# Expert products of a routed SwiGLU layer with the weights as the stationary operand

## What is computed

```python
T, D, F, E, TOP_K = 2048, 256, 1024, 8, 2
probs = softmax(x @ gate_w)                       # T x E
weights, experts = top_k(probs, TOP_K); weights /= weights.sum(-1)
for i in range(E):
    wi = where(experts == i, weights, 0).sum(-1)
    h = silu(x @ w1[i]) * (x @ w3[i])             # T x F
    out += (h @ w2[i]) * wi[..., None]
```

## Time and profile before

| | |
|---|---|
| runs | 791.32, 793.56, 793.77 us; median 793.56 us |
| the profiled execution | 792.24 us, of which the span of instructions is 790.5 us |
| mean granted TensorE clock | 0.901 |
| routed tiles | from 420 us to 777 us of the span |

### The profile page before, as it was taken

How to read it: one execution, slowest core, us unless ns; L and a number is a source line. 1 busy time by engine, 2 the same in 40 slices (tenths; PEclk the granted TensorE clock), 3 DMA queues, 4 the chain that set the end, 5 groups by cost and what they waited for, 6 DMA issues and landing times.

```text
span 790.5 us, 16899 instructions
## 1 busy us (share of the span) xinstructions
PE 656.0 (83%) x4582; PEld 456.3 (58%) x4582; DVE 505.7 (64%) x1269; ACT 383.9 (49%) x894; POOL 277.6 (35%) x297
## 2 busy tenths in 40 slices
PE   3899999995765775577317999999999999999991
PEld 2788888873323335477313666666666666666661
DVE  6588999997687456688693464646464555564441
ACT  1466666655869335476224443645353545443320
POOL 3111111220354402544202363637364545563311
PEclk9899999998898997555557999999999999999997
DMA  9100000003000006111371514262434353512214
GB/s 283 37 14 13 13 14 14 7 0 106 2 0 0 1 9 230 30 34 27 127 247 29 187 28 139 77 182 47 135 81 133 83 147 81 188 28 35 35 15 119
DMA packets 45682, 58.89 MB, mean 74 GB/s; under 512 B 13296, under 2 KB 39216, under 8 KB 45328
## 3 DMA queue, kind: packets, MB, share of 16 engines
q1 hardware_dynamic: 38128, 47.79, 18.5%
q0 software_dynamic: 7488, 10.31, 7.5%
HBM read 145.90 MB, written 11.80 MB: 199 GB/s over the span
## 4 chain that ended last, share of the span: by engine, by line
PE 56%; DVE 18%; issue 10%; ACT 5%; DMA 4%; POOL 3%; DVEq 2%; ACTq 1%; SPq 0%; POOLq 0%
PE psum L1000 19%; PE psum L1022 10%; PE psum L708 4%; PE psum L1013 3%; PE psum L692 3%; PE psum L715 3%; PE psum L728 2%; ACT region L1271 2%; PE psum L697 1%; PE psum L747 1%; DMA region<-neg_max_dram 1%; PE psum L735 1%; DVE region L1893 1%; POOL region L590 1%; PE psum L891 1%
## 5 line engine op out<-in xcount | busy, mean ns | idle before, releaser
L1000 PE MATMUL psum<-region 128*128 x936 | 217.1, 382 | 1.0 <-DVE region L1889 1.0
L1000 PEld LDWEIGHTS psum<-region 128*128 128x128 bf16 x936 | 92.2, 98 | 96.5 <-issue 4.1
L1254 ACT ACTIVATE region<-psum 128x512 f32<-128x512 f32 x78 | 46.5, 596 | 182.0 <-PE psum L1000 182.0
L636 POOL DMA_INDIRECT sum_dram<-region,row_token x39 | 74.5, 1911 | 133.7 <-DVE region L1885 133.7
L1022 PE MATMUL psum<-region 128*128 x936 | 109.1, 273 | 5.6 <-DVE region L1893 5.6
L1022 PEld LDWEIGHTS psum<-region 128*128 128x128 bf16 x936 | 90.4, 98 | 18.8 <-issue 8.2
L1868 DVE TENSOR_TENSOR region<-psum,region 128x512 f32<-128x512 f32 x78 | 53.9, 691 | 69.9 <-ACT region L1254 69.8
L529 POOL TENSOR_TENSOR region<-region,pair_mask 128x256 f32<-128x256 f32 x32 | 21.3, 687 | 127.5 <-ACT region L1061 127.5
L628 POOL DMA_INDIRECT region<-xrow_dram,row_token x39 | 40.9, 1048 | 55.1 <-DVE row_token L1863 27.2
L1893 DVE TENSOR_TENSOR region<-psum,region 128x1024 bf16<-128x1024 f32 x39 | 47.6, 1222 | 17.7 <-ACT region L1262 17.7
L1347 DVE TENSOR_REDUCE region<-psum 128x8 f32<-128x1024 f32 x32 | 39.0, 1220 | 17.7 <-PE psum L708 17.7
(11 more groups left out here) (291 smaller groups left out, 1208.3 us busy)
## 6 DMA issues: line engine op xcount, KB each, us to landing
region<-in_L_ffn_w SPq DMA_DIRECT2D x117, 1024.0 KB
region<-in_ctx SPq DMA_DIRECT2D x32, 128.0 KB, 2.5
region<-neg_max_dram SPq DMA_DIRECT2D x2, 1536.0 KB, 9.8
xrow_dram<-region SPq DMA_DIRECT2D x1, 2080.0 KB, 8.3
x_sb<-in_x SPq DMA_DIRECT2D x4, 512.0 KB, 6.8
region<-in_ctx SPq DMA_DIRECT2D x2, 1024.0 KB, 6.9
sum_dram<-x_sb SPq DMA_DIRECT2D x1, 2048.0 KB, 7.5
region<-neg_max_dram SPq DMA_DIRECT2D x1, 768.0 KB, 5.8
```

Of the source, the lines that this page charges most:

```text
L636: pool.indirect_dma_start(sum_dram, bass.IndirectOffsetOnAxis(ap=row_token[:, t:t + 1], axis=0), y_d[:, t % 2, :], None, compute_op=ALU.ad ...
L1000: last = mm(psum[:, 2 * f + n, :], (xT_lo if xl else xT_hi)[:, p, k, :], weights_at(place, wl, n, k * F1 + f * FH, FH), start=(i == 0), st ...
L1254: act_fn(sil_d[:, f, :], psum[:, 2 * f, :], ACT.Silu).then_inc(sil_d_ready, 1)
```

## The change

The gate and up products swap their operands: a 128 x 128 block of the weights is stationary and the 128 tokens of the tile move. Each half of F is done in 4 blocks c of 128 hidden columns, so a half has 48 matmuls of 128 columns in place of 12 of 512, and the result comes out with the hidden dimension on the partitions: what was transposed before is so already. `h_transposes` goes. silu and the product with up work as before on 128 x 512. The product h_d goes to SBUF, now one buffer for each half; ScalarE and VectorE make its bf16 halves from SBUF per half layer (`h_high(t, f)`, `h_low(t, f)`), into a double-buffered `hT_pair`. Within a tile step `h_high(t, 0)` and `h_low(t, 0)` now stand ahead of `x_high` and `x_low`. `hidden_d` has a new wait for `h_low` of the same half of the tile before. `PAIRS` has its second and third pair swapped; in down, whose stationary operand is still hT, the order is hi, lo, hi.

```diff
-            (F32, 2, B), (F32, 2, ROW), (BF16, 2, KT, P), (BF16, 2, KT, P), (F32, 2, FH), (F32, 2, F1),
-            (BF16, F1 // P, P), (BF16, F1 // P, P), (F32, 2, D), (F32, NT),
+            (F32, 2, B), (F32, 2, ROW), (BF16, 2, KT, P), (BF16, 2, KT, P), (F32, 2, FH), (F32, 2, FH),
+            (BF16, 2, 2, F1 // P, P), (F32, 2, D), (F32, NT),
...
-            PAIRS = ((0, 0), (0, 1), (1, 0))
+            PAIRS = ((0, 0), (1, 0), (0, 1))
...
-                    for i, (k, (xl, wl)) in enumerate((k, pair) for k in range(KT) for pair in PAIRS):
-                        last = mm(psum[:, 2 * f + n, :], (xT_lo if xl else xT_hi)[:, p, k, :],
-                                  weights_at(place, wl, n, k * F1 + f * FH, FH), start=(i == 0), stop=(i == 3 * KT - 1))
+                    for c in range(FH // P):
+                        for i, (k, (xl, wl)) in enumerate((k, pair) for k in range(KT) for pair in PAIRS):
+                            last = mm(psum[:, 2 * f + n, c * P:(c + 1) * P], weights_at(place, wl, n, k * F1 + f * FH + c * P, P),
+                                      (xT_lo if xl else xT_hi)[:, p, k, :], start=(i == 0), stop=(i == 3 * KT - 1))
                 last.then_inc(gu_done, 1)
...
-            def h_transposes(t, p):
-                pe.wait_ge(h_d_ready, 2 * t + 2)
-                for f in range(F1 // P):
-                    last = tr(bank(4, F1 // P, P, count=2)[:, f, :], h_d[:, p, f * P:(f + 1) * P], ident[:])
-                last.then_inc(th_done, 1)
-
             def down_d(t, place):
-                pe.wait_ge(hT_low, t + 1)
+                p = t % 2
+                pe.wait_ge(hT_low, 2 * t + 2)
...
-                if t >= 1:
-                    h_transposes(t - 1, 1 - p)
-                else:
+                if t == 0:
                     x_transposes(1, 1)
...
-            h_transposes(NT - 1, 0)
             down_d(NT - 1, places[NT - 1])
...
-            def h_high(t):
-                act.wait_ge(th_done, t + 1)
-                act_fn(hT_hi, bank(4, F1 // P, P, count=2), ACT.Copy).then_inc(hT_high, 1)
+            def h_high(t, f):
+                act.wait_ge(h_d_ready, 2 * t + f + 1)
+                act_fn(half_of(hT_hi, t, f), h_d[:, f, :], ACT.Copy).then_inc(hT_high, 1)
...
                 silu_d(t, 0)
                 if t >= 1:
-                    h_high(t - 1)
+                    h_high(t - 1, 1)
...
                 silu_d(t, 1)
+                h_high(t, 0)
                 if 0 < t < NT - 1:
                     x_high(t + 1, 1 - p)
...
-                tt(h_d[:, p, f * FH:(f + 1) * FH], psum[:, 2 * f + 1, :], sil_d[:, f, :], ALU.mult).then_inc(h_d_ready, 1)
+                if t >= 1:
+                    dve.wait_ge(hT_low, 2 * (t - 1) + f + 1)
+                tt(h_d[:, f, :], psum[:, 2 * f + 1, :], sil_d[:, f, :], ALU.mult).then_inc(h_d_ready, 1)
...
-            def h_low(t):
-                dve.wait_ge(hT_high, t + 1)
-                tt(hT_lo, bank(4, F1 // P, P, count=2), hT_hi, ALU.subtract).then_inc(hT_low, 1)
+            def h_low(t, f):
+                dve.wait_ge(hT_high, 2 * t + f + 1)
+                tt(half_of(hT_lo, t, f), h_d[:, f, :], half_of(hT_hi, t, f), ALU.subtract).then_inc(hT_low, 1)
...
                 hidden_d(t, p, 0)
                 if t >= 1:
-                    h_low(t - 1)
+                    h_low(t - 1, 1)
                 if t == 0:
                     x_low(1, 1)
                 hidden_d(t, p, 1)
+                h_low(t, 0)
                 if 0 < t < NT - 1:
                     x_low(t + 1, 1 - p)
```

More of the change, by code:

```diff
@@ L187, in build @@
          iota_e, iota_t, tcmp, te, tchg, tcum, tslot, slots_f, xg, xT_hi, xT_lo, sil_d, h_d,
-         hT_hi, hT_lo, y_d, w_col, stage) = lay(
+         hT_pair, y_d, w_col, stage) = lay(
             region1,
@@ L202, in build @@
         tile_hot = sil[:].rearrange("p n c -> p (n c)").bitcast(BF16)[:, 0:TOP * B * NT].rearrange("p (i t) -> p i t", t=NT)
-        tile_num = h_d.rearrange("p n c -> p (n c)").bitcast(BF16)[:, 0:TOP * B * 2 * NT].rearrange("p (i n t) -> p i n t", n=2, t=NT)
+        hT_hi, hT_lo = hT_pair[:, 0, :, :, :], hT_pair[:, 1, :, :, :]
+        tile_num = hT_pair.rearrange("p a b c d -> p (a b c d)")[:, 0:TOP * B * 2 * NT].rearrange("p (i n t) -> p i n t", n=2, t=NT)
         sum_dram = nc.dram_tensor("sum_dram", (B * P + P, D), F32, kind="Internal").ap()
@@ L356, in build @@
         h_d_ready = sem("h_d_ready")
-        th_done = sem("th_done")
         hT_high = sem("hT_high")
@@ L1021, in down_d @@
                 for i, (f, (hl, wl)) in enumerate((f, pair) for f in range(F1 // P) for pair in PAIRS):
-                    last = mm(psum[:, 7, 0:D], (hT_lo if hl else hT_hi)[:, f, :], weights_at(place, wl, 2, f * D, D),
+                    last = mm(psum[:, 7, 0:D], (hT_lo if hl else hT_hi)[:, p, f, :], weights_at(place, wl, 2, f * D, D),
                               start=(i == 0), stop=(i == 3 * (F1 // P) - 1))
@@ L1258, in x_high, with half_of @@
                 act_fn(xT_hi[:, p, :, :], bank(6, 4, P)[:, 0:KT, :], ACT.Copy).then_inc(xT_high, 1)
-            def h_high(t):
-                act.wait_ge(th_done, t + 1)
-                act_fn(hT_hi, bank(4, F1 // P, P, count=2), ACT.Copy).then_inc(hT_high, 1)
+            def half_of(v, t, f):
+                return v[:, t % 2, f * FH // P:(f + 1) * FH // P, :].rearrange("p c n -> p (c n)")
+            def h_high(t, f):
+                act.wait_ge(h_d_ready, 2 * t + f + 1)
+                act_fn(half_of(hT_hi, t, f), h_d[:, f, :], ACT.Copy).then_inc(hT_high, 1)
             def weights_high(n, t, place, new):
@@ L1307, in _ @@
                 tile_step(t, t % 2, info)
-            h_high(NT - 1)
+            h_high(NT - 1, 1)
         @block.vector
@@ L1920, in _ @@
                 tile_step(t, t % 2, info)
-            h_low(NT - 1)
+            h_low(NT - 1, 1)
             weighted(NT - 1, 0)
```

## The result

The changed kernel takes 901.23 us (median of 4 runs, 899.99 to 906.83) against 793.66: 1.1375 times the kernel before, 95% interval 1.1322 to 1.1428. The profiled execution took 901.1 us, its span is 899.3. Forecast were 880 us and a range of 850 to 915.

A forecast was written before the change was run, and what follows sets the result against it. TensorE was taken to bound the routed stage, its queue's register instructions after the change. From 792.24 us: 38 tiles x 2.44 = +92.7, tile 0 +2.1, weight tiles -4.7, end -3.3, giving 879.0, forecast 880; range 850 to 915.

The forecast's parts named there:

- The deciding step: Gate and up on TensorE's queue: one register instruction per new weight address, 64 a tile at 125 ns, 8.00 us.
- The array term: Routed tile by the array alone: 5.34 + 0.22 + 2.62 = 8.18 us, 0.71 less than before.
- The lead: Tile's end: next tile's first register instruction comes 2.8 us after the last; array needs 3.0, so only queue lead is lost.
- The place register: Read of the next tile's place, mid second half of gate and up: no lead left to hide it, +0.65 us.
- a sign of being wrong: Head of the tile: the prediction is wrong if TensorE waits for VectorE there longer than 0.3 us.
- the 4.7 us of the weight tiles: Extra time of tiles that convert new weights: disappears in the slack, -4.7 us (bound: 0).
- Other edits: New wait, buffers, conversions per half and pair order: no extra cost; ScalarE and VectorE load totals stay about the same.
- the end: Last down product: follows in about 2.8 us in place of 6.14, -3.3 us.
- the array sets the pace: Rival for gate and up: register instructions overlap or are fewer; 8.18 us a tile, about 763 us; chance 0.06.
- the uncovered pair: Rival: the pair without its own register instruction costs the queue up to 56 ns, to 948 us; chance of over half 0.08.
- The granted clock: Rival: sparser streaming in gate and up drops the clock to 1.2 GHz, 15.9 us a tile, about 1060 us; chance 0.04.
- Faster register steps: Rival: register steps come faster in a dense stream, and the two effects about cancel; chance 0.03.

The follow-up runs named there:

- after_psum: The changed kernel with only the product h_d in PSUM banks 4 and 5 in place of SBUF: 894.94 us, 1.1253 times before.
- more_registers: The changed kernel with the second pair of each k at its own weight address, 96 register instructions a tile in place of 64: 1056.76 us.
- half_registers_psum: The changed kernel with three pairs of a k sharing one address (low weights left out), 32 register instructions a tile, and h_d in PSUM: 770.11 us.
- branch_on_slot: The changed kernel with gate and up written three times at fixed addresses, chosen by branches; h_d in PSUM, x conversions first, slot read behind down: 883.76 us.

## Why the prediction was right, and where it was short

**The deciding step held.** The prediction put one register instruction to each new weight address, 64 a tile, at 125 ns where the row says 46. The count is 64. The price was tried in both directions: 32 more cost 130 ns each, 32 fewer bring the ordinary tile to the array's bound. That the second pair on one address is free held too: three pairs and two register instructions come in some 260 ns, and most register instructions are 124 or 125 ns apart whether one pair or two lie between them.

**The array term held.** 8.18 us a tile without register instructions in gate and up, 8.26 measured; the transposes are gone and worth their 0.87, but only where the array is the bound.

**The lead.** That nothing new is lost but the lead held in an ordinary tile: a first register instruction 2.8 us after the last of the tile before was forecast, and the median in after is 2.72. The place register's 0.65 is 0.65 in the queue (0.77 from step to step, of which a step is 0.12) and shows as 0.56 of waiting on the array. In the 7 weight tiles the 2.72 is 3.7, and in the one shown under after_psum TensorE waits 0.63 us for VectorE at its head, over the 0.3 that the prediction named as a sign of being wrong.

**Where the other 22 us are** (901.1 in the profile against 879.0 in the sum):
- The 63 steps with the place came to 8.9 us (609.5 to 618.4) where 7.88 + 0.65 = 8.53 was forecast, so an ordinary tile took 11.66 (their median) and not 11.33: 37 tiles x 0.33 = 12. The excess has a pattern in the trace: from 450 us on, 1982 of 2248 steps are within 140 ns, nearly all of them 124 or 125, and 266, about every eighth, are longer, 186 in the mean. So 125 was right for the step by itself, and what was not forecast is the longer one in eight. more_registers has it in every eighth step too, though there 16 and not 24 loads and matmuls lie between eight steps, which speaks against a fetch of code after a fixed number of instructions. What it is stays open.
- The 7 weight tiles. The sum let the 4.7 us of the weight tiles disappear in the slack. Most of them did, as after_psum shows, where these tiles are 0.0 to 0.4 us over the others. But in after a new cost took their place: the tiles are 1.0 us longer than the others, some 7 us. The step that failed is in "Other edits", where moving the product from PSUM to SBUF was costed at nothing because the load totals stay the same. I read durations and not who else uses SBUF then. after_psum gives 5.5 us of the 7 back. The trace of before held the sign: there VectorE's own subtraction of weights, on SBUF alone, takes 2.29 us as a rule (the median), and 3.22 where GpSimd's subtraction has another 1.07 us to run when it starts:

```profile
624.85 3.81 POOL L654 TENSOR_TENSOR region<-region 128x2048 f32 x1
...
627.59 3.22 DVE L1850 TENSOR_TENSOR region<-region 128x2048 f32 x1 [0.16 <-issue]
```

- The stage began 2.2 us later (422.2 against 420.0), in code that the change does not touch, and the end gained 2.1 and not 3.3: the last down product follows 4.06 us behind the one before, waiting for h_low.

The Trainium skill (SBUF — State Buffer, "SBUF: two separate sides") says that VectorE and GpSimd share a pair of SBUF ports under an exclusive lock, and that a VectorE operation with two SBUF inputs blocks against a GpSimd operation that reads SBUF, until that one ends. The runs agree: 3.53 us, ending 0.55 us after GpSimd, with two SBUF inputs, 0.68 with one in PSUM. Read beside the change's new operands, it would have pointed at these 7 us before the run.

**The rivals.** That the array sets the pace was priced at 763 us; half_registers_psum, which takes both obstacles away, gives 770. That the uncovered pair costs up to 56 ns would make the tile 13.1 us and is out by its 11.66. The granted clock was 1.00 from 430 to 880 us in after, its level of 2.4 GHz, so that rival is out too. Faster register steps are out by the 124 ns, which are what line 853 had shown.

## What to carry to other kernels

Ahead of a swap of stationary and moving operand, count the addresses that are computed at run time and multiply by the distance of the queue's register instructions where they lie in the open, not by their duration; compare that with the columns they have to hide under. Long matmuls give the queue a lead that short ones can spend, so a mix of both forms can beat either. When an intermediate moves from PSUM to SBUF, look at which engines read SBUF at that time.

## What the runs showed of the hardware

- A register instruction of TensorE's queue shows 46 ns and holds the queue for 124 ns, 131 in the mean with a longer step in every eighth; 16 a tile were free under 24 matmuls of 512 columns, 64 set the pace under 96 of 128.
- Compare-and-branch instructions of that queue took from 65 ns to 5.8 us in branch_on_slot. Of the 13 ways out of the first body over the two others, 11 took 1.9 to 4.5 us and 2 took 0.3 to 0.4.
- VectorE on two SBUF operands, 0.68 us by itself, took up to 3.85 us while GpSimd worked from SBUF.
- The granted clock was 0.89 in the mean from 450 to 980 us in more_registers, part of the time at its lower level of 1.2 GHz, and the tiles stayed alike; in after it was 1.00.
